# The second layer's first matrix product in six column parts in place of three

## The reference

```
x = x + layer1(layernorm(x))   # each token's id picks one of 4 matrices C (512 x 512):
                               # silu(h C^T) * (h C^T), times C again
x = x + layer2(layernorm(x))   # 8 experts of 64 hidden units, the best 2 of a softmax router weigh them
   gated = silu(h gate_w) * (h up_w)          # 8 x 64 = 512 hidden columns each
   out   = sum_e w_e * gated_e down_w_e  +  sum_e w_e * (h lora_A_e) lora_B_e    # rank 16 each
```

## Time and profile before

| what | value |
|---|---|
| median of 3 runs | 335.31 us |
| lowest and highest run | 333.41 us, 335.71 us |
| span of the profiled execution, first to last instruction | 331.4 us |
| TensorE busy (matmul / weight load) | 305.7 us, 92% / 270.0 us, 81% |
| VectorE busy | 213.3 us, 64% |
| ScalarE busy | 82.9 us, 25% |
| GpSimd busy | 108.5 us, 33% |

### The profile page before, as it was taken

The page is one execution under the profiler, slowest core; times in us unless marked ns, Lnnn a source line. Parts: engine busy times, 40 slices in busy tenths (PEclk is TensorE's granted clock), DMA queues, the critical chain, the costliest instruction groups (busy, mean ns, idle before and its releaser), DMA issues.

```text
span 331.4 us, 5376 instructions
## 1 busy us (share of the span) xinstructions
PE 305.7 (92%) x1636; PEld 270.0 (81%) x1637; DVE 213.3 (64%) x603; ACT 82.9 (25%) x158; POOL 108.5 (33%) x118
## 2 busy tenths in 40 slices
PE   1668997999999999999999999999999999999990
PEld 1645885888888888889999999999999999999970
DVE  6789854665576466557766685658656776657520
ACT  4432212332323233231212221221112121212110
POOL 1779734466655535431120111101110111011111
PEclk9999997999999999999999999999999999999996
DMA  7362784122212212211210112011100000000001
GB/s 283 133 215 69 202 312 186 63 65 95 96 63 95 95 63 84 106 63 64 65 53 10 63 63 63 3 60 63 63 26 37 32 32 32 0 32 34 32 26 40
DMA packets 8074, 26.37 MB, mean 80 GB/s; under 512 B 1408, under 2 KB 1408, under 8 KB 7424
## 3 DMA queue, kind: packets, MB, share of 16 engines
q0 software_dynamic: 4320, 14.16, 12.5%
q1 hardware_dynamic: 3744, 12.08, 10.8%
HBM read 17.06 MB, written 9.18 MB: 79 GB/s over the span
## 4 chain that ended last, share of the span: by engine, by line
PE 81%; POOL 7%; DMA 4%; issue 4%; DVE 2%; ACT 0%; DVEq 0%; SPq 0%; ACTq 0%; POOLq 0%
PE p_y L680 10%; PE p_y L681 10%; PE p_y L685 10%; PE p_h L680 7%; PE p_h L685 7%; PE p_h L681 7%; PE p_aT L675 5%; PE p_xT L669 4%; PE p_a L680 4%; PE p_a L681 3%; PE p_a L685 3%; PE p_b L681 3%; PE p_b L685 3%; PE p_b L680 3%; POOL xin L239 2%
## 5 line engine op out<-in xcount | busy, mean ns | idle before, releaser
L491 DVE TENSOR_TENSOR aT_lo<-p_aT,aT_hi 128x512 fp32r<-128x512 f32 (+1 forms) x35 | 26.3, 752 | 87.3 <-ACT aT_hi L319 84.5
L252 POOL DMA_INDIRECT out<-xout,out_row x16 | 16.6, 1036 | 135.0 <-DVE xout L499 133.2
L319 ACT ACTIVATE aT_hi<-p_aT 128x512 fp32r<-128x512 f32 (+1 forms) x35 | 22.7, 647 | 107.5 <-PE p_aT L675 101.6
L252 POOL DMA_INDIRECT x_rows<-xout,x_row x19 | 19.7, 1038 | 56.5 <-DVE xout L499 56.2
L680 PE MATMUL p_y<-ctx_hi,aT_hi 128*128 x76 | 32.1, 422 | 2.4 <-DVE xout L499 2.3
L681 PE MATMUL p_y<-ctx_lo,aT_hi 128*128 x76 | 30.7, 403 | 0.0
L680 PE MATMUL p_y<-w_hi,aT_hi 128*128 128x512 f32 x75 | 30.6, 408 | 0.0
L680 PE MATMUL p_h<-ctx_hi,xT_hi 128*128 x72 | 29.9, 415 | 0.0
L681 PE MATMUL p_y<-w_lo,aT_hi 128*128 128x512 f32 x75 | 29.4, 392 | 0.0
L681 PE MATMUL p_h<-ctx_lo,xT_hi 128*128 x72 | 28.2, 392 | 0.0
L246 POOL TENSOR_TENSOR rstd<-var_eps,neg_half 128x1 f32<-128x1 f32 x35 | 23.0, 656 | 12.8 <-DVE var_eps L474 10.8
(11 more groups left out here) (145 smaller groups left out, 663.5 us busy)
## 6 DMA issues: line engine op xcount, KB each, us to landing
stage<-ctx_t SPq DMA_DIRECT2D x4, 1024.0 KB, 6.0
xin<-x_rows SPq DMA_DIRECT2D x16, 256.0 KB, 2.6
stage<-w_up SPq DMA_DIRECT2D x4, 580.0 KB
stage<-w_down SPq DMA_DIRECT2D x1, 1280.0 KB
xin<-x,gather_row POOLq DMA_INDIRECT x19, 3.4
x_rows<-xout,x_row POOLq DMA_INDIRECT x19
out<-xout,out_row POOLq DMA_INDIRECT x16
ids<-token_ids SPq DMA_DIRECT2D x1, 8.0 KB, 1.6
```

The costliest lines, as they stand in the source:

```text
L252: nc.gpsimd.indirect_dma_start(out=to, out_offset=bass.IndirectOffsetOnAxis(ap=rows, axis=0), in_=xout[:, r % 2, :], in_offset=None).then_ ...
L319: nc.scalar.activation(aT_hi[:, 0:cols], p_aT[:, 0:cols], ACT.Copy).then_inc(ahi_ready, 1)
L491: nc.vector.tensor_tensor(aT_lo[:, 0:cols], p_aT[:, 0:cols], aT_hi[:, 0:cols].bitcast(F32), ALU.subtract).then_inc(alo_ready, 1)
```

## The change

Inside `l2_first` each of the three parts is cut in two halves of columns: part a into 196 + 196, parts b and c into 192 + 192. Each half runs its own 8 matmuls of `hi_passes` and 4 of `lo_passes`, the second half after the first, in the same PSUM bank. The part's semaphore is raised by the last matmul of its second half. A tile of layer 2 so has 72 matmuls in its first product in place of 36, over the same 1160 columns, each still with a weight load of its own.

```diff
-                    w = up_part(c0, c1)
-                    hi_passes(to[:, 0:c1 - c0], xT_hi, KB, *w)
-                    pe.wait_ge(xlo_ready, r + 1)
-                    lo_passes(to[:, 0:c1 - c0], xT_lo, KB, w[0]).then_inc(ready, 1)
+                    cm = c0 + (c1 - c0) // 2
+                    for b0, b1 in ((c0, cm), (cm, c1)):
+                        w = up_part(b0, b1)
+                        hi_passes(to[:, b0 - c0:b1 - c0], xT_hi, KB, *w)
+                        pe.wait_ge(xlo_ready, r + 1)
+                        last = lo_passes(to[:, b0 - c0:b1 - c0], xT_lo, KB, w[0])
+                    last.then_inc(ready, 1)
```

## The result

The changed kernel takes 359.6 us (median of 3 runs, 358.11 to 361.37) where the kernel before took 335.31 us (333.41 to 335.71): a ratio of 1.078, 95% interval 1.072 to 1.085. Two of the ten runs of one experiment (three parts, 96 columns) were over 1.5% above its fastest and count as slow; ratios are worked out without them. The forecast was 362.6 us, from 356 to 376.

A forecast was written before the change was run, and what follows sets the result against it. TensorE, never idle in layer 2, was taken as the bound. At 112 ns each, 72 matmuls take 8.06 us for 6.36; +1.70 us x 16 tiles = +27.3 us on 335.3 gives 362.6 us, range 356 to 376.

The forecast's parts named there:

- TensorE bounds layer 2: Layer 2 but its tail: TensorE is busy every microsecond and alone in the chain, a step of 10.79 us.
- 112 ns a matmul, from the dummy products: First product: twelve 128-column float32 matmuls start 112 ns apart, held by weight loads; 72 such give 8.06 us, +27.3 us.
- the 16-bit products: Matmuls of 16 columns starting under 43 ns apart, a sign that neither handing out nor accumulating into one bank sets 112 ns.
- around the span: Outside the profile's span: the three runs' median, 335.31 us, lies 3.9 us above the 331.4 us span, and that stays.
- The waits cost nothing: Layer 2's waits for `xT_lo`, `act`, `aT_hi`, `aT_lo` and `xout` add nothing; `act` has 1.65 us of cover.
- Streaming alone: Between matmuls of a part, the next load hides at any width: 88 to 95 ns, 335 to 344 us; chance 0.10.
- three readings: Streaming time at 192 columns: 88 ns proportional to 384, 91 on a line through 384 and 512, 95 with a fixed part.
- The reading with a fixed 15 ns: Streaming in the first product: one column per 2.4 GHz cycle plus 15 ns, so 95 ns at 192 columns.
- The longer load (157 ns): First product: float32r loads occupy 48 ns more than transposes' loads, so 157 ns a matmul, +79 us, 414 us; chance 0.03.
- the lower clock: Layer 2: shorter matmuls drop TensorE to 1.2 GHz, 213 ns a matmul, +143 us, 478 us or more; chance 0.02.
- handing out: First product: 72 matmuls in a row drain TensorE's queue, 124 to 132 ns each, 376 to 386 us; chance 0.05.
- The formula of the Trainium skill: First product: N/2.4 + 2.5 ns a matmul, 82.5 and 84.2 ns at 192 and 196 columns, a sum of -6.1 us.

The follow-up runs named there:

- three parts, 96 columns: Kernel before, its three parts kept, with 96 of 128 stationary columns from layer 2's second tile on: 332.88 us, ratio 0.997.
- the narrower blocks: Changed kernel with only 96 or 112 of 128 stationary columns in the first product from layer 2's second tile on: 337.87 and 344.03 us.
- the repeated one: Changed kernel run again, unchanged, on the second chip beside the second half of the experiments: 358.68 us against 333.22 us, ratio 1.076.
- Part c alone: Against the kernel before, only part c cut into two halves of 192 columns, parts a and b in one piece: 341.5 us, ratio 1.023.
- the uneven cuts: Changed kernel with each part cut at column 320 or at column 256 instead of the middle: 379.88 and 364.72 us.
- 256 + 128: Changed kernel with part a cut into 256 + 136 columns, parts b and c into a 256 and a 128 piece: 364.72 us, ratio 1.092.
- at 96 columns: Changed kernel, six even parts, with 96 of 128 stationary columns in the first product from layer 2's second tile on: 337.87 us, ratio 1.015.
- nine parts: Changed kernel with each part cut in three pieces of 128 to 132 columns, 108 matmuls a step: 422.89 us, ratio 1.268.
- 320 + 64: Changed kernel with part a cut into 320 + 72 columns, parts b and c into a 320 and a 64 piece: 379.88 us, ratio 1.137.

## Why the prediction was right

**TensorE bounds layer 2**: held. It is without idle time from 147.5 us to the tail in both profiles, and all that was added showed in the span: from the first matmul of part a to the end it is 183.8 us before (147.6 to 331.4) and 210.6 after (149.0 to 359.6), +26.8.

**112 ns a matmul, from the dummy products**: held. Steady loads are 112 to 113 ns apart, the first product is 8.02 us for the 8.06 forecast, the step 12.46 for 12.5. Sixteen steps at +1.67 us are +26.7, for +27.3. The pace is all but the same at 192 and 196 columns, as expected of a load. That the weight load is what takes 112 ns was an argument then; the narrower blocks, with the 16-bit products, show it.

**The measured difference of the medians**, +24.3 us and +25.5 us on the second chip, lies somewhat under the steps' +26.7. Both intervals hold it: 7.0% to 8.1% of 333.22 us is 23.4 to 27.0 us, and 7.2% to 8.5% of 335.31 is 24.0 to 28.5. The rest is not resolved by these runs. Part of the spread lies in layer 1, which the change leaves alone: the spans of the first two profiles differ by 28.2 us, and 1.4 of this lie ahead of layer 2 (149.0 for 147.6). The first tile's high products took longer in the second of them (`p_a` from `ctx_hi`, four matmuls, duration ns min/median/max, first and last start; before, then after):

```profile
L680 PE MATMUL p_a<-ctx_hi,xT_hi x4: 389/395/494, 21.1 to 22.6; 128*128 x4
L680 PE MATMUL p_a<-ctx_hi,xT_hi x4: 628/628/789, 21.7 to 24.4; 128*128 x4
```

The granted clock of 17 to 26 us was 1.00 in the one profile and 0.69 in the other, and 0.81 in the repeated one. My 3.9 us "around the span" was of this kind too: the profiled executions after have 1.8 us around the span (361.37 and 359.6), so the execution profiled before would have taken about 333.2 us, less than any of the three timed. It did not enter the forecast, which added the sum to the median.

**The waits cost nothing**: held. The timeline that answers to the earlier trace rows:

```profile
243.63 0.60 PE L669 MATMUL p_xT<-ident,xn 128*128 128x128 f32 x4
...
244.43 0.69 DVE L556 TENSOR_TENSOR act<-silu,up_gated 128x512 f32<-128x512 f32 x1 [1.17 <-ACT silu L331]
...
247.30 0.70 PEld L675 LDWEIGHTS p_aT<-ident,act 128*128 128x128 f32 x5
```

VectorE now waits 1.17 us for part c's silu, because its router work is done in the longer first product; `act` is ready at 245.12 and its reader starts at 247.30, 2.18 us of cover for 1.65 before. Part c alone, at a third of the loss, says the same.

**Streaming alone**: the rival did not come true, but its sizes can now be read, since the narrow blocks laid it bare: 90 ns (6.46 / 72) for the mix of 192 and 196 columns, and from the uneven cuts 118 ns at 256 and (13.73 - 4.43) / 36 - 112 = 146 at 320. Of my three readings, proportional to 384 columns gives 88, 117 and 146, and the straight line through 384 and 512 gives 92, 119 and 147; both are within 2 ns, and the runs do not choose between them. The reading with a fixed 15 ns, which I took into the forecast as "about 95" and into the expectations, gives 96, 122 and 148, too long by 2 to 6 ns. That is a part of the misses at 256 + 128 (368 us expected, 364.7 measured) and at 96 columns (345 and 337.9); another part is that I added to 335.3 us, where the kernel before took 334.0 and 333.22 beside these runs. The forecast did not depend on it, as 112 was larger than any of the readings.

**The longer load (157 ns), the lower clock, handing out**: none came. The load record's 48 ns over that of a transpose are not occupancy: a 192 ns record repeats every 112 ns. The granted clock was 1.00 from 147.5 to 346 us, and nine parts in a row kept 111 ns, with a half longer row of short matmuls than the change has. The clock column alone would not settle it. For 12.0 to 15.2 us of the kernel before it reads 1.00 too, columns as in the earlier trace rows:

```profile
12.00:15.20 3.20, 3.20 (x16) 3.20 (x17) 2.85 (x6) 1.02 (x1) 2.46 (x2) 1.00 0.23 61
```

Yet the dummy products then ran at some 213 ns. What settles it is the second product, which kept its 231 ns a matmul.

**The formula of the Trainium skill** ("TensorE: Matmul & The Clock Gate", Back-to-back issue gap), which the page gives for a matmul by itself and which would have led to -6.1 us, counts only the streaming: 82.5 ns at 192 columns. The trace has 112 there with full blocks and 90 with 96 columns.

The same page of the Trainium skill (LDWEIGHTS (loading the stationary operand)) gives a load P / 1.2 ns for P columns; worked out as an estimate from it, 107, 93 and 80 ns for 128, 112 and 96. The trace agrees within 5 ns at 128 and 112 columns (112 and 98); at 96 it shows only that the load takes no more than 90.

No version better than the kernel before came out of this. The widest piece that this kernel writes with one matmul is 512 columns; at that width 1160 columns still need three parts, and at 384 columns the load is hidden with 63 ns to spare (175 less 112).

## What to carry to other kernels

With `float32r` operands, price a matmul as the larger of two numbers: the streaming of its moving columns (here 7 + 0.4375 x N ns, the line through 175 at 384 and 231 at 512, within 2 ns of what 192 to 320 columns measured) and the load of the next stationary block (here 112 ns for 128 columns). By this estimate they cross at about 240 moving columns. A piece narrower than that costs the whole load, however narrow it is, so the uneven cuts cost more than the even one. Cutting into pieces that are all wider costs some 5 to 7 ns for each matmul added, by estimate (7 is the constant of the line, and 2 x 118 less 231 is 5); no run here did that. To find the load's price in a trace that has no short matmul of the kind, look at the distance of two loads at the border from transposes to the product, and do not read it off the load's own record.

## What the hardware showed beside this

The recorded duration of a load is longer than its period, and by different amounts: 192 ns with a period of 112 at 128 columns, 0.18 us with 98 at 112 columns, 0.16 us with no more than 90 at 96 columns, 140 ns with 109 for the transposes. Only the distance from one to the next is a price. And the first 72-column matmul after a long one is followed by the next after 0.03 us (230.97 and 231.00 in the 320 + 64 timeline), though the load for this next one began only at 230.97. With 112 ns for a load, the recorded start lies some 0.08 us ahead of the time when the weights are there, by estimate, as in the earlier trace rows.
